# Thirty-six transposes of the identity at the head of TensorE's program

## The reference

```
x = x + tanh(g_xattn[0]) * wkv(time_decay, time_first, k=layernorm(x), v=ctx)   # a recurrence along the 128 steps
x = x + tanh(g_ffn[0])   * ffn(layernorm(x))       # silu(z Wg * s) * (z Wu * s) Wd, 704 wide
x = x + tanh(g_xattn[1]) * attention(layernorm(x), ctx)   # 16 heads of 8
x = x + tanh(g_ffn[1])   * experts(layernorm(x))   # 8 experts of 352, and one shared
```

## Time and profile before

| what | value |
|---|---|
| three runs | 509.40, 510.41 and 509.39 us, median 509.40 us |
| profiled execution | 509.36 us |
| its span, from the first to the last instruction | 507.6 us |
| PE busy | 474.1 us, 93% of the span |
| DVE busy | 381.3 us, 75% |
| ACT, POOL busy | 244.9 us, 230.1 us |

### The profile page before, as it was taken

How to read it: one execution, slowest core, us unless ns; L and a number is a source line. 1 busy time by engine, 2 the same in 40 slices (tenths; PEclk the granted TensorE clock), 3 DMA queues, 4 the chain that set the end, 5 groups by cost and what they waited for, 6 DMA issues and landing times. The chain is left out here.

```text
span 507.6 us, 10286 instructions
## 1 busy us (share of the span) xinstructions
PE 474.1 (93%) x3384; PEld 259.3 (51%) x3384; DVE 381.3 (75%) x765; ACT 244.9 (48%) x461; POOL 230.1 (45%) x319
## 2 busy tenths in 40 slices
PE   2998999998999999999999998998999999999993
PEld 2663664854733633343343333333445647788882
DVE  4989889899888789999999999998465633333321
ACT  2761232332232078889999998787412010233331
POOL 3736434154755355867677763213010660042433
PEclk9999999999999999999999999999999999999998
DMA  7750175002775116566566655300022224378843
GB/s 237 216 176 0 43 166 89 2 0 62 186 195 150 54 57 174 147 171 184 162 163 172 171 153 147 84 5 5 1 94 77 74 94 166 120 185 195 192 112 41
DMA packets 67256, 59.96 MB, mean 118 GB/s; under 512 B 10048, under 2 KB 62256, under 8 KB 67216
## 3 DMA queue, kind: packets, MB, share of 16 engines
q1 hardware_dynamic: 63712, 55.24, 39.6%
q0 software_dynamic: 3072, 4.21, 4.9%
q10 hardware_dynamic: 432, 0.00, 0.0%
HBM read 38.90 MB, written 22.50 MB: 121 GB/s over the span
## 5 line engine op out<-in xcount | busy, mean ns | idle before, releaser
L1325 DVE TENSOR_REDUCE MX<-psum 128x2 f32<-128x512 f32 x256 | 162.1, 682 | 10.0 <-PE psum L1190 8.4
L1374 ACT ACTIVATE HP<-psum 128x512 f32<-128x512 f32 x224 | 122.1, 602 | 28.9 <-PE psum L1205 26.4
L1190 PE MATMUL psum<-QKA 60*128 60x256 bf16 x512 | 81.3, 273 | 7.1 <-DVE MX L1325 5.6
L1205 PE MATMUL psum<-QKA 60*128 60x256 bf16 x512 | 81.1, 273 | 1.5 <-DMA QKA<-max_scr 1.0
L1291 PE MATMUL psum<-HP,VP 128*32 128x256 f32 x1024 | 81.8, 391 | 0.3 <-issue 0.2
L602 PE MATMUL psum<-space_a,space_w 128*128 128x512 f32 x160 | 73.1, 602 | 1.9 <-DVE HP L629 1.9
L1190 PEld LDWEIGHTS psum<-QKA 60*128 60x128 bf16 x512 | 31.6, 94 | 63.8 <-DVE MX L1325 44.6
L1966 POOL DMA_INDIRECT out_x<-OE,to_u x16 | 24.9, 1557 | 62.6 <-ACT OE L2001 60.1
L602 PEld LDWEIGHTS psum<-space_a,space_w 128*128 128x128 f32 x160 | 29.0, 190 | 36.5 <-issue 31.0
L2089 PE MATMUL psum<-XT,WE 128*128 128x256 f32 (+1 forms) x192 | 44.0, 379 | 0.9 <-ACT XT L1985 0.9
L199 PE MATMUL psum<-space_a,wsh 128*128 128x512 f32 (+1 forms) x96 | 43.6, 598 | 0.3 <-PEq L1497 0.3
(11 more groups left out here) (207 smaller groups left out, 767.3 us busy)
## 6 DMA issues: line engine op xcount, KB each, us to landing
QKA<-stack_scr SPq DMA_DIRECT2D x32, 480.0 KB, 4.5
stack_scr<-PARTS SPq DMA_DIRECT2D x32, 192.0 KB, 2.1
WE<-in_W SPq DMA_DIRECT2D x16, 352.0 KB, 4.0
stack_scr<-PARTS SPq DMA_DIRECT2D x32, 128.0 KB, 2.0
XD<-dispatched SPq DMA_DIRECT2D x8, 258.0 KB, 3.9
X<-in_x SPq DMA_DIRECT2D x4, 512.0 KB, 5.8
CTX<-in_ctx SPq DMA_DIRECT2D x4, 512.0 KB, 8.2
MB<-in_mask SPq DMA_DIRECT2D x16, 128.0 KB, 3.3
```

Of the source, the lines that this page charges most:

```text
L1190: return pe.matmul(to[:, tt * T:(tt + 1) * T], QKA[rows, k, 0, h, tt * P:(tt + 1) * P], QKA[rows, k, 1, h, :], start=True, stop=True)
L1205: return pe.matmul(to[:, (m % 2) * T:(m % 2 + 1) * T], QKA[rows, k, 1, h, st * P:(st + 1) * P], QKA[rows, k, 0, h, :], start=True, stop=True)
L1325: dve.tensor_reduce(MX[:, par, head_of(n), :], src[:, :].rearrange("p (a s) -> p a s", a=2), axis=AX.X, op=ALU.max).then_inc(a_red, 1)
L1374: act.activation(PT[:, i % 2, st, 2 * half:2 * half + 2, :].rearrange("p j t -> p (j t)"), TBK3[THIRDS[m]], ACT.Exp).then_inc(a_exp, 1)
```

## The change

PE's program gets 36 transposes between its wait for the identity and its first transpose of a normalised tile. Each has the identity as its input and writes the first 128 columns of bank 7 (`KV[1]`), which nothing reads before unit 1 of the keys and values writes it anew. They signal no semaphore and wait for none.

```diff
@@
             N_GATES, N_SMALL, N_ROWS = 2, 9, 14
+            WARM = 36
@@
                 def _(pe):
                     pe.wait_ge(s_id, 1)
+                    for n in range(WARM):
+                        pe.transpose(KV[1][:, 0:P], ident[:], ident[:])
 
                     pe_wkv_in(pe, 0, 0)
                     pe_wkv_in(pe, 0, 1, WB2)
```

## The result

The changed kernel is slower: 514.15 us median of six runs (511.2 to 514.67) against 509.41 us (509.26 to 510.41) in six runs of the kernel before, a ratio of 1.0082 with a 95% interval of 1.0057 to 1.0106. The profiled execution took 514.67 us, and its span is 512.9 us where it was 507.6, 5.3 us more. The forecast was 508.7 us.

What follows compares the result with a forecast made beforehand. PE is busiest overall (474.1 of 507.6 us), but at the head it idles until 10.04 us, then works at half pace. A 0.7 us gain at x1 gave 509.36 - 0.7 = 508.66, predicted 508.7 us; range 508.0 to 510.4.

Steps and rivals of the forecast that it cites:

- The 36 transposes fit into the idle time and cost nothing themselves: PE's head: they start at about 3.0 us, end at 10.0 just when Z1 comes, and no engine waits for them.
- Rival A: PE's head: transposes don't raise the clock, so the chain is 0.7 us later, 510.1 us, or 510.9; chance 0.25.
- 6.6: Rival A's threshold: 690 ns of overrun at 105 ns saved by each fast transpose; stated as fewer than six running fast.
- C: Rival: the gain is the full one on PE, 1.0 to 1.3 us, giving 508.2 us; chance 0.08.
- faster: Outcome of more than 0.2% faster: rival C and a tenth or so of the forecast; chance given as 0.16.
- The first tiles gain 0.49 us: First four transposes take 0.60 us instead of 1.09, so EB, PA and DVE's chain come 0.49 us earlier.
- The keys and values; PE goes on at the fast pace behind its wait for group 1: Group 1 starts at 15.6 us instead of 16.85; 1.28 us gained on PE, shrinking to 0.7 at x1.
- The rest: no transfer holds an absolute time, so the gain is kept: Behind x1: everything follows earlier, L602 at about 33.6 instead of 34.30 us, and the 0.7 us lasts to the end.

Runs made afterwards that it cites:

- run 3: Changed kernel plus 14 more identity transposes in PE's 1.65 us wait for group 1's tiles; 509.69 us, ratio 1.0008 to the kernel before.
- run 2: Changed kernel plus 184 increments of an unused semaphore on PE, 256 instructions added in all; 532.23 us, ratio 1.0454 to the kernel before.
- run 4: The kernel of run 3 plus 156 increments of an unused semaphore, 256 instructions added in all; 529.37 us, ratio 1.0384 to the kernel before.
- run 6: Kernel before plus 50 transposes of only 16 rows at the head, 100 instructions, clock low there; 510.33 us, ratio 1.0020.
- run 7: Changed kernel's 36 whole transposes divided, 26 at the head and 10 in PE's wait for group 1; 513.52 us, ratio 1.0083 to the kernel before.
- run 8: Kernel before plus 4 ordinary matmuls on zeros at the head and 2 in the wait for group 1, 24 instructions; 508.70 us, ratio 0.9987.
- run 1: Changed kernel with 36 transposes of only 16 rows in place of the whole ones; 512.66 us, ratio 1.0068 to the kernel before.
- run 5: Kernel before plus 18 transposes of only 16 rows at the head, 36 instructions; 509.21 us, ratio 0.9996.

## Why the prediction was wrong

- *The 36 transposes fit into the idle time and cost nothing themselves*: right. They took 7.00 us where 7.0 were worked out, and PE's first real transpose stood at 10.02 instead of 10.04 us. That it was 7.0 to the tenth is partly luck: the same 36 took 6.43 us in run 3, 6.20 in run 2 and 6.80 in run 4, since the clock rises after more or fewer of them.
- *Rival A, transposes don't raise the clock*: wrong. Their lengths in the changed kernel go from 421 to 272 ns while nothing else has run on PE:

```profile
L1006 PE MATMUL psum<-ident x36: 272/421/476, 3.0 to 9.8; 128*128 128x128 f32 x36
```

  The Trainium skill, page TensorE: Matmul & The Clock Gate, section Part 4: PE-mode transpose, says that full rate does not engage in transpose mode. This trace, with float32 transposes, disagrees: 36 of them alone brought the fast pace.
- *Two sums of the prediction are slightly off.* By its 6.6, rival A needs fewer than seven fast transposes, not fewer than six. And C with a tenth of the forecast gives a chance of about 0.14 for "faster", not 0.16. Neither changes the forecast.
- *The first tiles gain 0.49 us*: nearly right. PA starts at 12.17 us (12.13 forecast), EB at 10.80 (10.76), so 0.45 us.
- *The keys and values; PE goes on at the fast pace behind its wait for group 1*: this step failed. I worked out the wait itself (13.8 to 15.6 us), and argued from a pause of 0.60 us ahead of 24.16 us that a pause leaves the pace. A pause of 1.65 us did not, although PE had worked for 10.9 us without one before it: the clock was down from about 15.8 to 19.2 us, and the gain of 0.7 became a loss of 0.4 us. Why it fell at this pause and not at the longer one of 1.89 us in run 6 stays open, so the runs give no length of pause that is safe. Runs 3, 7 and 8, which fill the pause, give the 0.7 us back (L602 at 33.58, 33.62 and 33.55, forecast 33.6).
- *The rest: no transfer holds an absolute time, so the gain is kept*: this failed most dearly, and put at nothing what cost 4.7 us. I looked only at SP's transfers near the head. The kernel before already had a wait of PE for a transfer on this way, the 1.0 us for the maxima. And the code is a transfer too; the packet that matters there moves with the number of instructions ahead. At 72 instructions it meets the store of the maxima, costs 1.5 us directly and 1.4 us through the clock that falls in the longer wait. Runs 1, 2, 5 and 7 show it for this term: the loss is there at 72 and at no other count, whether the head is warm or not.
- *The term at WE* (1.8 us) is less well settled. It appears with 72 instructions in two of three profiles and with 100 in one of two, a packet of code lying in its stretch each time; none with 0, 24, 36 and 256. That the packet delays that load is argued from this, and wasn't seen packet by packet as at the maxima. Nor does the count alone place it, as run 7 shows. So this term stays open.
- The late waits differ from execution to execution (run 1: 512.0 to 515.8 us), so the sum of terms holds for the profiled execution, and the medians say which kernel is faster.

## What to carry to other kernels

Here the warm-up paid only with few, wide instructions (run 8). Warm TensorE in its idle time in this way, and follow the first long wait behind the warm-up: unless that is filled too, the clock can fall there and cost more than the early rise brought. When instructions are added or removed on an engine with a long straight program, compare the packets of kind "instruction" with the transfers on the path, in both traces, and test the place of the code by itself with instructions that do almost nothing. A small edit whose cost appears hundreds of microseconds behind it, at a wait for a transfer, is the sign of this.

## What the runs showed of the hardware

- A store of 24 KB in small packets took 2.8 to 3.1 us instead of 1.5 where a packet of 16 KB of code (1.1 to 1.5 us long in the three) came among them.
- Semaphore increments in a row on TensorE took about 0.15 us each: 28 fewer in run 4 than in run 2 brought the real work forward by 4.36 us. I had taken them for nearly free.
- Matmuls on zeros raised the clock too: behind the four of run 8 the first real transposes took 0.66 us, not 1.09.
- Waits of PE of 1.65 and 2.5 us had the low clock at their end or just behind it (changed kernel), and one of 1.89 us did not (run 6).
- The granted clock in the view by windows reads 1.00 ahead of the first change that the record has, also where the durations show the lower level.
